# Counting edges of a graph layer with one-hot products: two chunks to a pair, groups of 256 edges, twelve pairs to a batch

## The chip, the core and the metric

The kernel runs on one core of one Trainium2 chip. The metric is the time of one execution on the device in microseconds (us). Before the change three runs gave 567.61, 568.38 and 569.0 us, median 568.38. One more execution was recorded by the hardware profiler; it took 568.89 us, of which 567.1 us are the span that the profile shows.

## The reference

Four residual layers over 1250 nodes with 512 values each: an attention layer over a graph, a gated dense layer, a convolution over the same graph, and a mixture of eight experts. Only the first step matters here. The two graph layers share 40000 edges, whose targets come sorted:

```
dst = minimum(int(1250 * uniform(40000) ** 2.0), 9999);  src = randint(40000, 0, 1250)
order = argsort(dst, stable=True);  src = src[order];  dst = dst[order]
# layer 1: segment softmax over the edges of each target, weighted sum of Wx[src] by target
# layer 3: segment_sum(norm * h[row], col) with the edges and one loop per node
```

The kernel never visits edges again after it has turned them into a matrix C of counts, C[source, target] = how many edges join the two. Both graph layers are then dense products with C.

## The kernel before

Nodes stand in T = 10 tiles of 128 rows (NP = 1280). C has 1280 by 1280 counts in float16, kept in two halves, `C` and `C2`, that take turns and are added at the end of the stage.

**Groups, windows, pairs.** The sorted edges are cut into NG = 105 groups of GE = 384 edges, one group per partition. Targets are cut into NW = 80 windows of WN = 16 targets. As both are sorted, a group meets few windows: there are at most NG + NW - 1 = 184 = NPAIR meetings of a group and a window. Each is a *pair*. A pair has CH = 3 *chunks* of 128 edges. For each chunk VectorE makes a one-hot matrix of the source's low seven bits (128 wide, `L_ring`) and one of source tile and target within the window (RW = 160 wide, `R_ring`). TensorE multiplies them (`count`, line 1445): three products into one PSUM bank. A fourth matmul, the *merge* (line 1452), with the identity as weights, adds what `C` or `C2` holds at that window already. ScalarE writes the sum back (the *write*, line 555). The window's place is a value in a register, different for each pair.

**Order and waits.** Pairs come in batches of LB = 8, 23 batches (NB). The one-hots of a batch (24 chunks) are made in two halves and stand in a ring of two batches. Pair k writes `C` when k is even and `C2` when odd, so merge k waits for the write of pair k-2 (line 1455; `written` counts the writes). `count` of pair k waits, in TensorE's instruction queue, for the write of pair k-3, since three banks take turns (line 1443). In each batch, after the count of pair LB-2, TensorE loads the next batch's windows into registers (line 1520), and ScalarE does so after the write of pair LB-3 (line 606), both in `targets` (line 294).

**What else runs in the stage.** `BEGIN` starts one tile of layer norm in each of batches 1 to 10. Its steps are spread over the next batches: statistics and scale on VectorE (lines 839 to 857), normalization on ScalarE (530, at k = 1), four transposes on TensorE (1356, at k = 2), the copy to float16 on ScalarE (522, at k = 3), the low part on VectorE (862), and then the projection of the attention layer, 12 steps of two matmuls (1402 with 512 columns and 1403 with 16), placed between pairs by `LIN_SLOTS` in batches 3 to 12. VectorE evacuates the result (882, 884). In batches 12 to 15 the weights of the third layer are transposed (1417), copied (628) and split (989). Batch 16 transposes the thresholds of the softmax (1425). Batches 19 and 20 change ScalarE's function tables (lines 542 and 610). In batch 0 small products for the attention scores (1473, 1466) stand between pairs.

**How the pairs are found.** `pair_tables` (VectorE) turns each group's first and last window into selection masks `inside`, `inside_T` and `wneg` over the 184 pairs; `pair_matmuls` (TensorE, lines 1435 to 1439) multiplies the groups' edge values by these masks, so that each partition gets its edge of each pair. ScalarE (line 580) and VectorE (line 930) bring the tables `loT` and `qT` to SBUF. TensorE then transposes weights of layer 1, runs eight matmuls on zeros, and starts to count.

The stage ends when ScalarE has written all pairs and signals `hist_done`; the attention proper starts from that.

Of the kernel before, what the change touches and what calls it, by code (L numbers as in the profile page):

```python
# [22 lines left out]
CH = 3  # L23
GE = CH * P
NG = (EDGES + GE - 1) // GE
GLAST = EDGES - (NG - 1) * GE
# [3 lines left out]
NPAIR = NG + NW - 1  # L30
LB = 8
# [25 lines left out]
LIN_SLOTS = ((0,), (1, 2), (), (3, 4), (5, 6), (7,), (8, 9), (10, 11))  # L57
B_GW = max(BEGIN) + 2
B_CS = B_GW + K
# [6 lines left out]
def gnn_ffn_kernel(nc, x_d, src_d, dst_d, Ws_d, Wb_d, aw_d, ab_d, Wg_d, bg_d, We_d, be_d, gW_d, gb_d,  # L66
                   Wr_d, br_d, W1_d, b1_d, W2_d, b2_d, out_d):
    ctx = ExitStack()
    with ctx:
# [70 lines left out]
        dst_i, o = carve(big, 0, [GE], I32)  # L140
        hi_i, o = carve(big, o, [GE], I32)
# [8 lines left out]
        from_, o = carve(mid, o, [NPAIR])  # L150
        tv, o = carve(mid, o, [NPAIR])
        inside, o = carve(mid, o, [NPAIR], F16)
        inside_T, o = carve(mid, o, [NPAIR], F16)
        wneg, o = carve(mid, o, [NPAIR], F16)
        iota_lo, o = carve(mid, o, [P], F16)
        iota_q, o = carve(mid, o, [RW], F16)
        dst16, o = carve(mid, o, [GE], F16)
        ones16, o = carve(mid, o, [P], F16)
        span_i, o = carve(mid, o, [2], I32)
        num_words = num[:, :, :].rearrange("p h f -> p (h f)")  # L160
        lo16, o = carve(num_words, 0, [GE], F16)
        hi16, o = carve(num_words, o, [GE], F16)
        src_i = be_bc[:, 0:GE].bitcast(I32)
# [59 lines left out]
        ll, at = carve(small, at, [T, H])  # L223
        e1t, at = carve(small, at, [T, H])
# [6 lines left out]
        grp, at = carve(small, at, [8])  # L231
        kt, at = carve(small, at, [MAXPASS])
# [42 lines left out]

        def table_banks(j):

            return (bank[2], bank[3]) if j < 2 else (bank[6], bank[7])
# [42 lines left out]
        def _(sp):  # L321
            sp.wait_ge(sem("pads"), 2)
            full = (NG - 1) * GE
            for i_d, i_sb in ((src_d, src_i), (dst_d, dst_i)):
                sp.dma_start(i_sb[0:NG - 1, :], i_d[0:full].rearrange("(g e) -> g e", e=GE)).then_inc(sem("ld_edges"), 16)
                sp.dma_start(i_sb[NG - 1:NG, 0:GLAST], i_d[full:EDGES].rearrange("(g e) -> g e", g=1)).then_inc(sem("ld_edges"), 16)
# [88 lines left out]
        def _(g):  # L415

            nc.gpsimd.memset(src_i[96:NG, :], 0).then_inc(sem("pads"), 1)
            nc.gpsimd.memset(dst_i[96:NG, :], NP).then_inc(sem("pads"), 1)
# [13 lines left out]
            nc.gpsimd.memset(ones16, 1.0)  # L432
# [79 lines left out]
        def _(a):  # L512
# [63 lines left out]
            def lo_table(p):  # L576

                a.wait_ge(sem("table_psum"), p + 1)
                for n, j in ((2, 0), (1, 2)):
                    ins = act(loT.rearrange("p (k j) c -> p k j c", j=CH)[:, :, j:j + n, :],  # L580
                              bc(table_banks(j)[0][:, 0:NPAIR * n].rearrange("p (j k) -> p k j", j=n), [P, NPAIR, n, 2]), ACT.Copy)
                ins.then_inc(sem("lo_table"), 1)
# [14 lines left out]
            for b in range(NB):  # L597
# [3 lines left out]
                def middle(k):  # L601
# [9 lines left out]
                    if k == 3 and b - 1 in BEGIN:  # L611
# [214 lines left out]
        def _(v):  # L826
# [41 lines left out]
            gp = slice(0, NG)  # L868
            V.tensor_reduce(span_i[gp, 0:1], dst_i[gp, :], AX.X, ALU.min)
            link(V.tensor_reduce(span_i[gp, 1:2], dst_i[gp, :], AX.X, ALU.max))  # L870
            link(V.tensor_scalar(span_i[gp, :], span_i[gp, :], int(math.log2(WN)), None, ALU.logical_shift_right))
            V.tensor_copy(grp[gp, 0:2], span_i[gp, :])
            link(V.tensor_scalar(grp[gp, 2:3], span_i[gp, 1:2], float(NW - 1), 1.0, ALU.min, ALU.add))
            V.tensor_tensor(grp[gp, 2:3], grp[gp, 2:3], grp[gp, 0:1], ALU.subtract).then_inc(sem("n_ready"), 1)
# [476 lines left out]
        def _(pe):  # L1351
# [124 lines left out]
            def between(b, k):  # L1476
# [12 lines left out]
                if k == LB - 2:  # L1489
                    if b - B_GW in range(K):  # L1490
                        second_weights(b - B_GW)
                    if b == B_CS:
                        thresholds()
# [331 lines left out]
```

## Time and profile before

| | |
|---|---|
| median of the runs | 568.38 us (567.61 to 569.0) |
| profiled execution | 568.89 us, its span 567.1 us |
| TensorE matmuls (PE) | 501.0 us busy, 88% |
| VectorE (DVE) | 473.7 us busy, 84% |
| ScalarE (ACT) | 342.2 us busy, 60% |
| one-hots (line 940) | 100 instructions, 92.1 us |
| products (line 1445) | 552 matmuls, 248 ns each |
| merges (line 1452) | shown in one group as 92, 305 ns each; the other 92 stand in a group of their own |

How to read it: busy times are summed over the whole span. A matmul's shown length is its latency; matmuls start sooner than the one before has ended, so a rate is read from the distance of two starts. PEld is the loading of weights. "q" behind an engine's name means its instruction queue. Times of the rows below are us from the start of the span.

### The profile page before, as it was taken

How to read it: one execution, taken by the hardware profiler on the slowest of the kernel's cores; microseconds unless marked ns; L12 is line 12 of the kernel's file. 1: busy time of each engine (PE TensorE's matmuls, PEld its weight loads, DVE VectorE, ACT ScalarE, POOL GpSimd, SP SyncE). 2: the span in 40 equal slices, each digit the busy share in tenths (PEclk: the TensorE clock that was granted, in tenths of full speed). 3: DMA queues.
4: the chain of work that ended last, by engine and by line, in shares of the span. 5: the costliest groups of instructions: out<-in, count | busy, mean ns of one | idle time of the engine just before them, and what ended most of it. 6: DMA issues, size and time to landing. Idle time of an engine off the chain costs nothing.

```text
span 567.1 us, 12112 instructions
## 1 busy us (share of the span) xinstructions
PE 501.0 (88%) x4629; PEld 371.2 (65%) x4630; DVE 473.7 (84%) x933; ACT 342.2 (60%) x662; POOL 72.8 (13%) x83
## 2 busy tenths in 40 slices
PE   1879999887589999999899899989899998899995
PEld 1767777666488888888677544544466696566652
DVE  7999999799899999995898748995877786967681
ACT  5365555567889999994675523344435548756730
POOL 3000000000000000000000020123243410222342
PEclk9989999999899999999999979999999999999999
DMA  7970000002001111100000077000001129675111
GB/s 179 359 273 2 1 2 1 2 10 88 3 39 57 49 49 48 49 3 1 1 1 2 0 253 285 1 1 1 3 21 58 57 65 371 233 248 205 60 52 51
DMA packets 25306, 45.14 MB, mean 80 GB/s; under 512 B 6961, under 2 KB 7205, under 8 KB 25248
## 3 DMA queue, kind: packets, MB, share of 16 engines
q1 hardware_dynamic: 23264, 39.16, 20.2%
q0 software_dynamic: 1952, 5.18, 2.5%
q8 instruction: 39, 0.64, 0.5%
q14 instruction: 19, 0.16, 0.1%
q10 hardware_dynamic: 32, 0.01, 0.0%
HBM read 33.23 MB, written 11.95 MB: 80 GB/s over the span
## 4 chain that ended last, share of the span: by engine, by line
PE 48%; DVE 34%; issue 8%; DMA 4%; ACT 3%; POOL 1%; ACTq 0%; POOLq 0%; DVEq 0%
PE bank L1378 7%; PE bank L1643 5%; PE bank L1767 5%; PE bank L1402 5%; PE bank L1445 4%; DVE work L1072 4%; DVE big L940 4%; PE bank L1452 4%; PE bank L1356 3%; PE bank L1549 3%; PE bank L1562 2%; PE bank L1738 2%; DMA aux<-xperm_scratch 2%; DMA out<-aux 2%; DVE rings L1072 2%
## 5 line engine op out<-in xcount | busy, mean ns | idle before, releaser
L940 DVE TENSOR_TENSOR big<-mid 128x1536 f16<-128x1536 f16 (+1 forms) x100 | 92.1, 980 | 0.4 <-PE bank L1452 0.4
L1445 PE MATMUL bank<-big 128*128 128x160 f16 x552 | 72.1, 248 | 4.4 <-DVE big L940 4.4
L1549 PE MATMUL bank<-big,work 128*128 128x130 f16 x1080 | 67.4, 224 | 8.4 <-DVE work L1072 8.4
L1549 PEld LDWEIGHTS bank<-big,work 128*128 128x128 f16 x1080 | 64.3, 100 | 10.4 <-DVE work L1072 4.9
L1445 PEld LDWEIGHTS bank<-big 128*128 128x128 f16 x552 | 51.7, 111 | 7.0 <-DVE big L940 6.5
L656 ACT ACTIVATE mid<-aux,small 128x1280 f16<-128x1280 f32 x36 | 47.3, 1349 | 0.7 <-DVE work L1072 0.4
L1562 PE MATMUL bank<-big,mid 128*128 128x260 f16 x400 | 47.1, 275 | 0.1
L1643 PE MATMUL bank<-mid 128*128 128x512 f16 x200 | 47.2, 379 | 0.0
L555 ACT ACTIVATE big<-bank 128x160 f32 x92 | 27.9, 303 | 26.7 <-PE bank L1452 25.3
L555 ACT ACTIVATE mid<-bank 128x160 f32 x92 | 27.7, 302 | 25.6 <-PE bank L1452 24.2
L1562 PEld LDWEIGHTS bank<-big,mid 128*128 128x128 f16 x400 | 38.2, 96 | 7.5 <-issue 0.3
L517 ACT ACTIVATE sd<-ve 128x1 f32<-128x1 f32 x40 | 8.0, 200 | 52.8 <-DVE ve L841 52.8
L1402 PE MATMUL bank<-big,rings 128*128 128x512 f16 x120 | 38.6, 378 | 0.0
L472 POOL DMA_INDIRECT out<-aux x16 | 26.3, 1647 | 74.1 <-DVE aux L1294 71.7
L839 DVE BATCH_NORM_STATS2 st<-row 128x6 f32<-128x512 f32 x40 | 27.7, 691 | 8.5 <-POOL row L488 7.8
L1452 PE MATMUL bank<-mid,ident 128*128 x92 | 28.0, 305 | 7.6 <-ACT big L555 4.1
L1549 PE MATMUL bank<-big,rings 128*128 128x130 f16 x520 | 32.0, 220 | 2.5 <-DVE rings L1072 1.6
L530 ACT ACTIVATE rings<-row,nm,rs 128x512 f32<-128x512 f32 x30 | 24.3, 810 | 13.6 <-DVE nm L857 13.6
L1549 PEld LDWEIGHTS bank<-big,rings 128*128 128x128 f16 x520 | 29.9, 98 | 3.6 <-DVE rings L1072 1.9
L456 POOL TENSOR_TENSOR mid<-mid,ident 128x128 f16<-128x128 f16 x10 | 3.9, 424 | 215.9 <-DVE small L1126 215.9
L1643 PEld LDWEIGHTS bank<-mid 128*128 128x128 f16 x200 | 19.7, 104 | 18.1
L1356 PE MATMUL bank<-ident,rings 128*128 128x128 f32 x120 | 19.5, 286 | 12.3 <-ACT rings L530 7.9
(310 smaller groups left out, 1122.1 us busy)
## 6 DMA issues: line engine op xcount, KB each, us to landing
big<-in_L_ffn_W SPq DMA_DIRECT2D x10, 1024.0 KB, 11.0
mid<-in_L_ffn_W SPq DMA_DIRECT2D x6, 1024.0 KB, 13.0
xperm_scratch<-work SPq DMA_DIRECT2D x1, 5753.0 KB, 20.3
aux<-thr_scratch SPq DMA_DIRECT2D x8, 640.0 KB, 3.7
aux<-xperm_scratch SPq DMA_DIRECT2D x8, 523.0 KB, 4.0
row<-in_x SPq DMA_DIRECT2D x1, 2304.0 KB
aux<-in_L_gnn_Ws SPq DMA_DIRECT2D x4, 256.0 KB, 4.5
work<-in_L_gnn_W SPq DMA_DIRECT2D x1, 1024.0 KB, 13.8
```

What stands on the lines that cost most here:

```text
L555: ins = act(counts_at(at[k], k), count_bank(base, k)[:, 0:RW].rearrange("p (d s) -> p s d", s=T), ACT.Copy)
L656: act(zmask[i % NZ], thr_bc[:, h % 2, :], ACT.Sigmoid, bias=steep[:, s, h:h + 1], scale=-STEEP).then_inc(sem("z_made"), 1)
L940: return V.tensor_tensor(out.rearrange("p c (v two) -> p c v two", two=2), values.rearrange("p (v two) -> p v two", two=2).unsqueeze(1).to ...
L1072: V.tensor_tensor(weighted[i % NC], zmask[m % NZ], C[:, s, :], ALU.mult).then_inc(sem("cz_made"), 1)
L1356: ins = nc.tensor.transpose(b[:, k * P:(k + 1) * P], src[:, k * P:(k + 1) * P], ident[:, :])
L1378: ins = mm(out, xt16[:, xp, k, :], w16[:, wp, k, :], start=i == 0 and k == 0, stop=i == 2 and k == K - 1)
L1402: mm(bank[2 + t % 2][:, :], xt, W016[:, wp, k, :], start=j == 0, stop=last)
L1445: mm(count_bank(base, k)[:, 0:RW], L_ring[:, slot, k * CH + j, :], R_ring[:, slot, k * CH + j, :], start=j == 0, stop=False)
L1452: ins = mm(count_bank(base, k)[:, 0:RW].rearrange("p (d s) -> p s d", s=T), ident16[:, :], counts_at(at[k], k), start=False, stop=True)
L1549: ins = mm(acc_region(h, t), weighted[i % NC][:, t * P:(t + 1) * P], VP[:, s, part, h, :, :].rearrange("p b f -> p (b f)"), start=False, s ...
L1562: ins = mm(bank[2 * (t % 2) + g2][:, 0:4 * FE].rearrange("p (h f) -> p h f", f=FE), C[:, s, t * P:(t + 1) * P], VP[:, s, part, 4 * g2:4 * ...
L1643: ins = mm(bank[6 + t % 2][:, :], C[:, s, t * P:(t + 1) * P], hp[:, s, part, :], start=s == 0 and part == 0, stop=s == T - 1 and part == 1)
```

## The change

A group now has 256 edges and two groups stand side by side on one partition (79 partitions, NG = 158). A pair has two chunks. There are 158 + 80 - 1 = 237 pairs, rounded up to 240, in 20 batches of 12. A batch still has 24 chunks, so each instruction that makes one-hots has the shape of before. The masks have a second axis for the two groups of a partition, and each table product is made in two steps, one for each.

```
-CH = 3                                 +CH = 2
 GE = CH * P
-NG = (EDGES + GE - 1) // GE            +ROWE = 2 * GE
                                        +NROW = (EDGES + ROWE - 1) // ROWE
                                        +NG = 2 * NROW
-NPAIR = NG + NW - 1                    +NPAIR = (NG + NW - 1 + LB - 1) // LB * LB
-LB = 8                                 +LB = 12
-LIN_SLOTS = ((0,), (1, 2), (), (3, 4), (5, 6), (7,), (8, 9), (10, 11))
+LIN_SLOTS = ((0,), (1,), (2,), (3,), (), (4,), (5, 6), (7,), (8,), (9,), (10,), (11,))
-B_CS = B_GW + K                        +B_CS = B_GW + K - 1
```

Transposes of a tile move from k = 2 to k = 4, their copy from k = 3 to k = 5, and the thresholds from batch 16, k = 6, to batch 15, k = 4 (they no longer wait for the last split of weights). The loads of windows stay at LB - 3, now k = 9, and bring 12 values. The table code, cut to its core:

```
 def pair_matmuls(p):
     for j in range(CH):
-        mm(lo_ps[:, o], lo16[0:NG, e], inside[0:NG, :], start=True, stop=True)
-        mm(q_ps[:, o], dst16[0:NG, e], inside_T[0:NG, :], start=True, stop=False)
-        mm(q_ps[:, o], hi16[0:NG, e], inside[0:NG, :], start=False, stop=False)
-        mm(q_ps[:, o], ones16[0:NG, :], wneg[0:NG, :], start=False, stop=True)
+        for a in range(2):
+            mm(bank[2][:, o], lo16[gp, e[a]], inside[gp, a, :], start=a == 0, stop=a == 1)
+        for a in range(2):
+            mm(bank[3][:, o], dst16[gp, e[a]], inside_T[gp, a, :], start=a == 0, stop=False)
+            mm(bank[3][:, o], hi16[gp, e[a]], inside[gp, a, :], start=False, stop=False)
+            mm(bank[3][:, o], step16[gp, :], wins[gp, a, :], start=False, stop=a == 1)
 def pair_tables(p):
...
-    V.tensor_scalar(from_[gp, :], iotaK[gp, :], grp[gp, 3:4], None, ALU.is_ge)
+    for a in range(2):
+        V.tensor_scalar(from_[gp, a, :], iotaK[gp, :], first_p[gp, a:a + 1], None, ALU.is_ge)
-    V.scalar_tensor_tensor(inside[gp, :], iotaK[gp, :], grp[gp, 4:5], from_[gp, :], ALU.is_lt, ALU.mult)
+    for a in range(2):
+        V.scalar_tensor_tensor(inside[gp, a, :], iotaK[gp, :], end_p[gp, a:a + 1], from_[gp, a, :], ALU.is_lt, ALU.mult)
...
-    V.tensor_tensor(wneg[gp, :], tv[gp, :], inside[gp, :], ALU.mult)
+    for a in range(2):
+        V.scalar_tensor_tensor(wins[gp, a, :], iotaK[gp, :], off_w[gp, a:a + 1], inside[gp, a, :], ALU.add, ALU.mult)
```

The tables `loT` and `qT` are now brought over by one instruction each instead of two. Ring sizes, the write, the merge and `count` with its waits are as before.

## Rows read from the trace of the kernel before

**Rows 1.** Busy time by stretch: stretch, length, busy PE, PEld, DVE, ACT, POOL (instructions), granted clock, DMA.
```profile
28.50:31.50 3.00, 2.51 (x16) 1.96 (x14) 2.62 (x4) 1.49 (x4) 0.00 (x0) 0.56 1.05 369
41.00:104.40 63.40, 62.39 (x600) 46.45 (x599) 58.92 (x105) 34.96 (x108) 0.00 (x0) 1.00 0.01 2
129.00:147.20 18.20, 13.93 (x144) 11.58 (x144) 17.34 (x22) 13.88 (x44) 0.00 (x0) 1.00 0.12 39
```
**Rows 2.** Chain that ended last, two batches behind the projections: start, length, what.
```profile
115.87 3.87 DVE big L940 x4
...
120.35 3.87 DVE big L940 x4
```
**Rows 3.** Timeline, one batch with a projection, TensorE: start, length, engine, line, operation.
```profile
61.46 0.30 PE L1452 MATMUL bank<-mid,ident 128*128 x1
...
62.07 0.63 PE L1356 MATMUL bank<-ident,rings 128*128 128x128 f32 x4
...
62.53 0.30 PE L1452 MATMUL bank<-big,ident 128*128 x1
...
64.19 0.30 PE L1452 MATMUL bank<-big,ident 128*128 x1
64.28 0.41 PE L1445 MATMUL bank<-big 128*128 128x160 f16 x3
...
64.53 0.38 PE L1402 MATMUL bank<-big,rings 128*128 128x512 f16 x1
...
64.77 0.30 PE L1452 MATMUL bank<-mid,ident 128*128 x1
```
**Rows 4.** Timeline near the stage's end: merges on TensorE and writes on ScalarE.
```profile
142.48 0.30 PE L1452 MATMUL bank<-big,ident 128*128 x1
...
142.81 0.30 ACT L555 ACTIVATE big<-bank 128x160 f32 x1
143.39 0.31 PE L1452 MATMUL bank<-mid,ident 128*128 x1 [0.40 <-ACT big L555]
...
143.73 0.30 ACT L555 ACTIVATE mid<-bank 128x160 f32 x1 [0.61 <-PE bank L1452]
...
144.09 0.31 PE L1452 MATMUL bank<-mid,ident 128*128 x1
```
**Rows 5.** Register loads by line: ns min/median/max, first and last start.
```profile
L294 PEldq TENSOR_LOAD <-mid x23: 587/591/1881, 20.9 to 142.6; - x23
L1522 PEldq TENSOR_LOAD <-small x1: 306/306/306, 146.5 to 146.5; - x1
L294 PEldq TENSOR_LOAD <-mid x1: 592/592/592, 63.3 to 63.3; - x1
```
**Rows 6.** Timeline, making the pair tables: VectorE's first step, first and twelfth table product.
```profile
10.82 0.16 DVE L916 TENSOR_TENSOR small<-small 105x1 f32<-105x1 f32 x1
...
12.85 0.31 PE L1435 MATMUL bank<-mid,num 105*128 105x184 f16 x1 [2.84 <-DVE mid L927]
...
14.49 0.36 PE L1438 MATMUL bank<-mid 105*128 105x184 f16 x1
```
**Rows 7.** Timeline: the merges that begin batches 0, 3 and 13, and the last one.
```profile
22.20 0.30 PE L1452 MATMUL bank<-mid,ident 128*128 x1
...
40.82 0.31 PE L1452 MATMUL bank<-mid,ident 128*128 x1
...
104.40 0.30 PE L1452 MATMUL bank<-mid,ident 128*128 x1
...
146.56 0.30 PE L1452 MATMUL bank<-big,ident 128*128 x1
```
**Rows 8.** Timeline: a weight copy on ScalarE, and the merges around a table change.
```profile
104.11 0.59 ACT L628 ACTIVATE mid<-bank 128x512 f16<-128x512 f32 x1
...
132.01 0.31 PE L1452 MATMUL bank<-mid,ident 128*128 x1
...
133.78 0.31 PE L1452 MATMUL bank<-big,ident 128*128 x1 [1.25 <-ACT big L555]
```

More of the change, by code:

```diff
@@ L22 @@
 EDGES = 40000
-CH = 3
+CH = 2
 GE = CH * P
-NG = (EDGES + GE - 1) // GE
-GLAST = EDGES - (NG - 1) * GE
+ROWE = 2 * GE
+NROW = (EDGES + ROWE - 1) // ROWE
+NG = 2 * NROW
+ELAST = EDGES - (NROW - 1) * ROWE
 WN = 16
@@ L29 @@
 RW = WN * T
-NPAIR = NG + NW - 1
-LB = 8
+LB = 12
+NPAIR = (NG + NW - 1 + LB - 1) // LB * LB
 LC = LB * CH
@@ L223, in gnn_ffn_kernel @@
         ll, at = carve(small, at, [T, H])
+        kt, _ = carve(small, at, [MAXPASS])
         e1t, at = carve(small, at, [T, H])
@@ L230, in gnn_ffn_kernel @@
         steep, at = carve(small, at, [T, H])
-        grp, at = carve(small, at, [8])
-        kt, at = carve(small, at, [MAXPASS])
+        w_lo, at = carve(small, at, [2])
+        w_hi, at = carve(small, at, [2])
+        n_win, at = carve(small, at, [2])
+        first_p, at = carve(small, at, [2])
+        end_p, at = carve(small, at, [2])
+        off_w, at = carve(small, at, [2])
+        n_pass, at = carve(small, at, [1])
         npass, at = carve(small, at, [1], I32)
@@ L578, in lo_table @@
                 a.wait_ge(sem("table_psum"), p + 1)
[L579 to L582, printed above, removed]
+                act(loT.rearrange("p (k j) c -> p k j c", j=CH), bc(bank[2][:, 0:NPAIR * CH].rearrange("p (j k) -> p k j", j=CH),
+                                                                    [P, NPAIR, CH, 2]), ACT.Copy).then_inc(sem("lo_table"), 1)
             for c in range(2):
@@ L610, in middle @@
                         act(sd[0:1, 0:1], zero16[0:1, 0:1], ACT.Sigmoid)
-                    if k == 3 and b - 1 in BEGIN:
+                    if k == 5 and b - 1 in BEGIN:
                         t = BEGIN[b - 1]
@@ L928, in pair_tables @@
+                for a in range(2):
+                    ins = V.scalar_tensor_tensor(wins[gp, a, :], iotaK[gp, :], off_w[gp, a:a + 1], inside[gp, a, :], ALU.add, ALU.mult)
+                ins.then_inc(sem("picks"), 1)
                 v.wait_ge(sem("table_psum"), p + 1)
-                for n, j in ((2, 0), (1, 2)):
-                    V.tensor_scalar(qT.rearrange("p (k j) c -> p k j c", j=CH)[:, :, j:j + n, :],
-                                    bc(table_banks(j)[1][:, 0:NPAIR * n].rearrange("p (j k) -> p k j", j=n), [P, NPAIR, n, 2]),
-                                    0.0, RW + 1.0, ALU.max, ALU.min)
+                V.tensor_scalar(qT.rearrange("p (k j) c -> p k j c", j=CH), bc(bank[3][:, 0:NPAIR * CH].rearrange("p (j k) -> p k j", j=CH),
+                                                                               [P, NPAIR, CH, 2]), 0.0, RW + 1.0, ALU.max, ALU.min)
@@ L1387, in _ @@
             pe.wait_ge(sem("n_ready"), 1)
-            mm(bank[5][0:NG, 0:1], tri[0:NG, 0:NG], grp[0:NG, 2:3], start=True, stop=True)
-            mm(bank[4][0:1, NPAIR:NPAIR + 1], ones[0:NG, 0:1], grp[0:NG, 2:3], start=True, stop=True).then_inc(sem("rb_psum"), 1)
+            gp = slice(0, NROW)
+            for a in range(2):
+                mm(bank[5][gp, 0:1], tri[gp, gp], n_win[gp, a:a + 1], start=a == 0, stop=a == 1)
+            for a in range(2):
+                ins = mm(bank[4][0:1, NPAIR:NPAIR + 1], ones[gp, 0:1], n_win[gp, a:a + 1], start=a == 0, stop=a == 1)
+            ins.then_inc(sem("rb_psum"), 1)
             def lin_a(t, j):
@@ L1479, in between @@
                         lin_a(BEGIN[b - 2], j)
-                if k == 2 and b - 1 in BEGIN:
+                if k == 4 and b - 1 in BEGIN:
                     t = BEGIN[b - 1]
@@ L1488, in between @@
                     score_bias()
[L1489 to L1493, printed above, removed]
+                if k == 4 and b == B_CS:
+                    thresholds()
+                if k == LB - 2 and b - B_GW in range(K):
+                    second_weights(b - B_GW)
             pe.wait_ge(sem("a_spread"), 1)
```

94 lines of the change are left out of this document (47 added, 47 removed).

## The prediction

> **What bounds the kernel now.** I read the page's engine shares first, then the table of busy time by stretch, then the chain that ended last, then the timeline inside single batches. The change touches only the stage that ends at 147 us, so everything behind it counts at nothing: it starts later or earlier by what the stage gives. In the stage two engines are nearly full, which is why the shares alone decide nothing. In the stretch with projections TensorE is busy 62.39 of 63.40 us and VectorE 58.92 [rows 1]; the chain runs through TensorE. Ten batches take 104.40 - 40.82 = 63.58 us [rows 7]. Behind that TensorE's share falls and VectorE is full, 17.34 of 18.20 us [rows 1]; the chain is a row of one-hots, 3.87 us a batch, 4.48 from batch to batch where a weight split stands between [rows 2]. These ten batches take 146.56 - 104.40 = 42.2 us [rows 7].
>
> The reader should see a third limit that no share shows. A merge waits for the write of two pairs before. Merge at 143.39, write at 143.73, end at 144.03, next merge of the same half of C at 144.09 [rows 4]: 0.70 us for two pairs, 0.35 a pair, with no product in that loop. TensorE's own work is nearly as long: merge to first product 0.09, three products 0.25 (0.083 each), so 0.34 [rows 3]. The two limits coincide today. With two products TensorE's own work falls to 0.26, the loop stays at 0.35.
>
> **The change part by part.**
>
> *One-hots.* 23 batches of 3.87 us become 20: VectorE loses 11.6 us of work. That is worth something only where VectorE sets the pace.
>
> *Start.* VectorE turns 512 instead of 384 edges a partition in six instructions. I take 0.1 to 0.16 us each, the growth of 0.35 to 0.56 us instructions by a third, plus one more wait: +0.8. `pair_tables` took from 10.82 to 12.70 (1.9 us) [rows 6]; its instructions over 184 pairs become 240 wide and three of them double: I take +1.3 (bounds 0.9 and 1.9: nothing for width, and all of it doubled). The twelve products start 0.15 us apart, (14.49 - 12.85)/11 [rows 6]: 184 columns at 1.2 GHz. They become 16 of 240 columns, 0.20 each, and the one small product becomes two: 15 x 0.20 + 0.20 against 1.64, +1.6 (bounds 0.4, if the clock were at 2.4 GHz by then, and 1.9). Two evacuations that become one give back some 0.1. All this is a chain, since TensorE's weight transposes, warm-up and first count stand behind the products in its queue. Sum +3.6.
>
> *Batches 0 to 2.* 24 pairs become 36. Twelve more at the loop's 0.35 are 4.2; four pairs beside score products lose 0.08 each, and two later loads grow by 0.16 (next part). Sum +4.1 (bounds 3.1 with the 0.26 of two products, and 6 if the stretch at half clock, 0.56 granted [rows 1], takes in more pairs).
>
> *Ten batches with a projection.* They stay with TensorE. Four more merges at 0.09, as the number of products is the same: +0.37. The transposes now stand at k = 4; at k = 2 they came at 62.07, though merge and products from 61.46 end at 61.80, so they waited 0.27 for ScalarE's normalization [rows 3]. That wait goes: -0.27. The normalization now delays write 2 and by that merge 4: +0.1. Then the register loads. One value took 0.306 us, eight 0.591 [rows 5], so 0.041 a value and twelve 0.75. The load on TensorE can't begin before the wait of the count ahead of it is over: at 63.3 [rows 5], and the matmul behind the load started at 64.53 [rows 3], so there were 1.23 us for 0.59 plus 0.2 until the next matmul (142.6 + 0.59 against 143.39 [rows 4, 5]): 0.43 spare, nothing stalled. After the change two pairs with one projection step each (0.50) stand there instead of two with two (1.66 became 1.0, -0.66), and the load is 0.16 longer: 0.39 short. So +0.4 a batch, between 0 (TensorE's queue covers it) and 0.75. Sum a batch 0.37 - 0.27 + 0.1 + 0.4 = 0.6, ten batches +6.2, bounds 1 and 10.
>
> *The rest.* Seven batches instead of ten. VectorE would need 3.87 to 4.48 each. The loop needs 12 x 0.353, and the load: merge 142.48 to merge 143.39 is 0.91 instead of 0.35, so +0.56 now [rows 4], +0.72 with twelve values. That is 4.96 a batch, more than VectorE's: the loop is late next, not VectorE. Seven are 34.7, less 0.7 for the last, which loads nothing. Work that VectorE's lead hid now shows: the transposes of weights (0.46, as 62.07 to 62.53 [rows 3]) and ScalarE's copies (0.59 [rows 8]) delay the loop by some 0.3 and 0.5 in three batches, 2.7 with the copy at the border; the ten threshold transposes and their copies 1.9; and the two table changes, each 1.77 between merges instead of 0.35 [rows 8], 2.8. Sum 34.0 + 2.7 + 1.9 + 2.8 = 41.4, against 42.2: -0.8 (bounds -11.6, VectorE's three batches, and +3).
>
> The Trainium skill has a rule for the load in "Advanced Engine Details and Errata", section "Sequencer Loop": while the sequencer executes a control instruction, other engine instructions can be read and queued, and its section on queue depths gives TensorE 64 places. By that rule a load would be hidden everywhere. The rows agree where projections fill the queue and disagree behind them, where merges stand 0.91 apart. By the rule alone the sum would be 5 us lower.
>
> *Sum.* 3.6 + 4.1 + 6.2 - 0.8 = +13.1. The profiled execution took 568.89, so 582.0; the median lies 0.5 below it: **581.5 us**.
>
> **The rivals.**
>
> *A. The merge loop and the loads carry the stage, as above:* 581.5, own range 577 to 586. For it: the 0.70 us loop stands in rows without a product in it. Against: it was never longer than TensorE's own work, so it may be a little shorter than it looks.
>
> *B. VectorE goes on setting the pace (the other side).* If the wait of the merge is met early and TensorE runs two products and a merge in 0.26, a late batch needs 12 x 0.26 + 0.72 = 3.84, just under VectorE's 3.87, and the three batches are a full gain of 11.6. Batches 0 to 2 then cost 2.3, those with projections 2 (load hidden), the start 3.6: 568.4 - 3.7 = 564.7. It decides from a pitch under 0.29 us. For it: the two limits coincide, so the rows cannot separate them where nothing stalls. Against: after a stall, merge to write and write to merge are again 0.34 and 0.36 [rows 4].
>
> *C. The loads stay hidden beside projections.* Then these batches cost 0.2 each, and the time is 577.5. For it: today nothing stalls there. Against: the spare 0.43 is used up by the numbers above.
>
> *D. The clock falls.* TensorE idles a quarter of each late pair. Granted clock was 0.56 (the 1.2 GHz level) at 28.5 to 31.5 after a stretch of short products, though TensorE was shown busy [rows 1]. If the 84 late pairs ran at that level, with merges and products twice as long, some 0.13 a pair: +11, 592. For it: the streams get thinner. Against: 1.00 was granted at 129 to 147, with 13.93 of 18.20 us busy [rows 1].
>
> "TensorE: Matmul & The Clock Gate" in the Trainium skill, section "A second HAM failure mode: psum-queue depth-cycling", tells of a kernel whose short idle gaps between groups of matmuls, as it cycled through PSUM banks, made the clock swing between its two levels. Every late pair has such a gap after this change. By that rule D would come; in the trace gaps of 0.4 to 1.2 us between merges left the clock at 1.00.
>
> **How the numbers follow.** A 0.68, C 0.13, D 0.06, B 0.08 (of it 0.05 faster, 0.03 within the bound), and 0.05 for a mix with small loads and less at the start, about 573. Under A, C, D and the mix the time is above 570.1, slower by over 0.3% (1.7 us, about what a measurement of this kernel tells from no change). Slower 0.92, same 0.03, faster 0.05. The range of 8 in 10 takes in A and C and half the mix at the low end, and part of D: 573 to 587.
>
> **What would show it.** Right: one-hots 80 us in total instead of 92.1; merges 0.35 apart behind the projections and ScalarE's writes the releaser of TensorE's idle time; VectorE idle there; first merge at about 25.8, batch 3 at 48.4, batch 13 at 118.5, last merge at 159.5; the load 0.75 us long; late batches 5 us. Wrong: merges 0.26 to 0.29 apart, or VectorE without idle time in the last seven batches (B); batches with projections at 6.6 us and not 7.0 (C); a granted clock under 0.9 behind 118 us (D); a first merge before 24.5.

## The result, and the profile after

The changed kernel takes 588.23 us (median of four runs, 587.49 to 588.63), the one before, timed again beside it, 568.69 (567.61 to 570.79). The ratio on record is 1.0322, 95% interval 1.0289 to 1.0356: slower by 3.2%. (The two medians alone are 3.4% apart.) The forecast was 581.5 with a range of 573 to 587. The direction was right, and 19.5 us came where 13.1 were forecast.

The profiled execution took 588.63 us, its span is 586.9. The merges divide the stage in the same places as [rows 7]. Timeline of the kernel after, the merges that begin batches 0, 1, 3 and 13, and the last one:

```profile
27.68 0.47 PE L1462 MATMUL bank<-mid,ident 128*128 x1
...
42.47 0.42 PE L1462 MATMUL bank<-mid,ident 128*128 x1
...
55.34 0.31 PE L1462 MATMUL bank<-mid,ident 128*128 x1
...
126.31 0.30 PE L1462 MATMUL bank<-mid,ident 128*128 x1
...
166.95 0.30 PE L1462 MATMUL bank<-big,ident 128*128 x1
```

Against [rows 7] this gives a table, in us:

| stretch | before | after | difference | forecast |
|---|---|---|---|---|
| to the first merge | 22.20 | 27.68 | +5.48 | +3.6 |
| batches 0 to 2 | 18.62 | 27.66 | +9.04 | +4.1 |
| ten batches with projections | 63.58 | 70.97 | +7.39 | +6.2 |
| from batch 13 to the last merge | 42.16 | 40.64 | -1.52 | -0.8 |
| from there to the end of the span | 420.54 | 419.95 | -0.59 | 0 |

The forecast missed 6.7 us in sum, and the first two lines alone hold 6.8 of them. What happened there can be read in the timeline of TensorE, kernel after, from the last transposes to the second pair (start, length, line, tiles, count, idle time before and its releaser):

```profile
22.48 1.04 PE L1360 MATMUL bank<-ident,aux 128*128 128x128 f32 x8
27.46 0.43 PE L1455 MATMUL bank<-big 128*128 128x160 f16 x2 [3.95 <-issue]
...
27.87 0.56 PE L1455 MATMUL bank<-big 128*128 128x160 f16 x2
28.22 1.81 PE L1483 MATMUL bank<-aux,work 128*128 128x16 f32 x8
29.86 0.43 PE L1462 MATMUL bank<-big,ident 128*128 x1
```

"issue" means that no semaphore explains the 3.95 us. The register loads do. Those of the whole kernel after (ns min/median/max, first and last start):

```profile
L297 ACTq TENSOR_LOAD <-mid x20: 768/784/2931, 23.6 to 160.4; - x20
L297 PEldq TENSOR_LOAD <-mid x20: 843/852/3032, 24.4 to 160.2; - x20
```

The same view cut to 19 to 30 us leaves TensorE's first one alone:

```profile
L297 PEldq TENSOR_LOAD <-mid x1: 3032/3032/3032, 24.4 to 24.4; - x1
```

The median load answers [rows 5]: 0.852 us for twelve values on TensorE, 0.784 on ScalarE. The first one lasts from 24.4 to 27.4, and the first product starts at 27.46. The clock stands in the busy table of the kernel after (columns as in [rows 1]):

```profile
23.50:27.40 3.90, 0.02 (x1) 0.00 (x0) 3.73 (x11) 0.70 (x2) 0.00 (x0) 0.77 1.06 379
27.50:42.40 14.90, 14.69 (x78) 13.98 (x79) 5.25 (x8) 3.35 (x11) 0.00 (x0) 0.50 0.82 290
43.00:55.30 12.30, 8.71 (x74) 6.09 (x71) 11.37 (x20) 9.12 (x31) 0.00 (x0) 1.00 0.01 2
56.00:126.30 70.30, 67.67 (x637) 51.20 (x634) 57.52 (x100) 44.41 (x144) 0.00 (x0) 1.00 0.01 2
126.30:167.00 40.70, 32.01 (x274) 23.23 (x272) 30.15 (x44) 29.48 (x97) 0.99 (x1) 1.00 0.11 34
```

All of batch 0 runs at a granted clock of 0.50, the 1.2 GHz level. Added up in stretches of 0.25 us, the lower level lasts 17.1 us in this kernel and 3.4 us in the one before, the stretch of [rows 1]. DMA is full (1.06) in the same stretch: the 5.75 MB transfer that zeroes a scratch tensor (from `work` to `xperm_scratch`) begins before the counts and lasted to about 39 us.

In the last line VectorE is busy 30.15 of 40.70 us where it was full before. The chain of waits no longer runs through its one-hots but through TensorE and ScalarE. Timeline of TensorE, kernel after, late in the stage:

```profile
158.93 0.31 PE L1462 MATMUL bank<-mid,ident 128*128 x1
...
159.33 0.31 PE L1462 MATMUL bank<-big,ident 128*128 x1
...
159.63 0.31 PE L1462 MATMUL bank<-mid,ident 128*128 x1
...
160.04 0.31 PE L1462 MATMUL bank<-big,ident 128*128 x1
160.14 0.34 PE L1455 MATMUL bank<-big 128*128 128x160 f16 x2
161.16 0.31 PE L1462 MATMUL bank<-mid,ident 128*128 x1 [0.68 <-ACT big L558]
```

Two pairs take 0.70 us (158.93 to 159.63), 0.35 a pair, as forecast from [rows 4]. (The single distances are uneven, 0.30 and 0.40 here and 0.28 and 0.42 in most late batches, so only the sum of two is to be compared.) Where the load stands, the gap is 1.12 (0.91 in [rows 4]). The one-hots (page of the kernel after) are 80.5 us in 88 instructions, against 92.1, and now wait:

```profile
L944 DVE TENSOR_TENSOR big<-mid 128x1536 f16<-128x1536 f16 (+1 forms) x88 | 80.5, 969 | 11.7 <-PE bank L1462 11.7
```

### The profile page after: what moved, and what is told of

The parts are those of the page before. It is cut to its first block, busy times and chain, and to the rows that moved or that the text cites. A ratio compares the mean times of both kernels' runs of the same rounds, so it can differ in the third digit from the quotient of the medians.

```text
span 586.9 us, 12303 instructions
## 1 busy us (share of the span) xinstructions
PE 515.6 (88%) x4622; PEld 380.1 (65%) x4623; DVE 465.0 (79%) x922; ACT 356.5 (61%) x717; POOL 72.4 (12%) x83
## 3 DMA queue, kind: packets, MB, share of 16 engines
q1 hardware_dynamic: 23212, 39.16, 19.5%
## 4 chain that ended last, share of the span: by engine, by line
PE 56%; DVE 27%; issue 9%; ACT 4%; DMA 2%; POOL 1%; ACTq 0%; POOLq 0%; DVEq 0%
PE bank L1462 7%; PE bank L1382 7%; PE bank L1776 6%; PE bank L1652 5%; PE bank L1455 5%; PE bank L1410 5%; DVE work L1076 4%; PE bank L1747 3%; PE bank L1360 3%; PE bank L1558 3%; PE bank L1571 2%; DVE rings L1076 2%; DVE st L840 1%; DVE work L981 1%; PE bank L1371 1%
## 5 line engine op out<-in xcount | busy, mean ns | idle before, releaser
L944 DVE TENSOR_TENSOR big<-mid 128x1536 f16<-128x1536 f16 (+1 forms) x88 | 80.5, 969 | 11.7 <-PE bank L1462 11.7
L1455 PE MATMUL bank<-big 128*128 128x160 f16 x480 | 81.6, 259 | 3.9 <-issue 3.9
L558 ACT ACTIVATE mid<-bank 128x160 f32 x120 | 36.4, 303 | 32.0 <-PE bank L1462 28.3
L558 ACT ACTIVATE big<-bank 128x160 f32 x120 | 36.5, 304 | 23.2 <-PE bank L1462 22.5
L1462 PE MATMUL bank<-mid,ident 128*128 x120 | 37.4, 311 | 11.2 <-ACT big L558 5.6
L1410 PE MATMUL bank<-big,rings 128*128 128x512 f16 x120 | 44.1, 379 | 2.6 <-issue 2.6
L1462 PE MATMUL bank<-big,ident 128*128 x120 | 36.8, 307 | 1.3 <-ACT big L558 1.3
L533 ACT ACTIVATE rings<-row,nm,rs 128x512 f32<-128x512 f32 x30 | 24.3, 810 | 13.6 <-DVE nm L858 13.6
```

The costliest lines, as they stand in the source:

```text
L558: ins = act(counts_at(at[k], k), count_bank(base, k)[:, 0:RW].rearrange("p (d s) -> p s d", s=T), ACT.Copy)
L944: return V.tensor_tensor(out.rearrange("p c (v two) -> p c v two", two=2), values.rearrange("p (v two) -> p v two", two=2).unsqueeze(1).to ...
L1410: mm(bank[2 + t % 2][:, :], xt, W016[:, wp, k, :], start=j == 0, stop=last)
L1455: mm(count_bank(base, k)[:, 0:RW], L_ring[:, slot, k * CH + j, :], R_ring[:, slot, k * CH + j, :], start=j == 0, stop=False)
L1462: ins = mm(count_bank(base, k)[:, 0:RW].rearrange("p (d s) -> p s d", s=T), ident16[:, :], counts_at(at[k], k), start=False, stop=True)
```

## The experiments

Times of merges below are from the profiled executions, medians and ratios to the kernel before from the timed ones. `a_` stands for a variant of the kernel after, `b_` of the one before. The kernel before was timed again beside each group of variants, there at medians of 570.2 to 570.8 us, so ratios are compared and medians only roughly. A single profiled execution can also lie at the edge of its runs: the one of `a_warm` took 584.25 us where the other three took 586.25 to 587.71, the one of `b_gap` 580.96 where the others took 576.96 to 578.42.

### The late stretch: loop or loads

Four kernels, with part of the work left out. In `a_noloop` and `b_noloop` merges add zeros instead of C and wait for no write, so TensorE needs no register; ScalarE's write waits for the one two back. In `a_noload` the merge reads C at one fixed place, so TensorE loads nothing but waits as before. In `a_loadonly` only the first and last merge of a batch are real, so the loads stay and the loop goes.

```
 a_noloop, b_noloop:
-  ins = mm(count_bank(base, k)..., ident16[:, :], counts_at(at[k], k), ...)
+  ins = mm(count_bank(base, k)..., ident16[:, :], zero16[:, 0:RW]..., ...)
-  if isinstance(base, int) and base + k > 1:
-      ins.wait_op(sem("written"), base + k - 1, "sem-ge")
 and in the write, on ScalarE:
+  elif base + k >= 2:  a.wait_ge(sem("written"), base + k - 1)
 a_noload:
-  ... ident16[:, :], counts_at(at[k], k), ...
+  ... ident16[:, :], (C, C2)[k % 2][:, :, 0:WN], ...
 a_loadonly: as a_noloop, but only for 0 < k < LB - 1
```

> The changed kernel with the merge reading zeros instead of C and not waiting for the write of two pairs before (the sums over pairs of one window are left out; every matmul and write stays). Theory 1, the loop of merge and write carries the late stretch: merges fall from 0.353 to 0.29-0.31 apart (the three PSUM banks bind next), the late batches from 5.1 to some 4.3 us, time 579 to 583. Theory 2, TensorE's rate or the register loads carry it: merges stay 0.35 apart, 587 to 589.

> The same edit in the kernel of before, with its three products to a pair. Theory 1: the loop does not bind there, VectorE and TensorE do: 567 to 569, no change of note. Theory 2, the loop costs something with three products as well: 563 to 566.

> The changed kernel with every merge reading window 0 of its half of C, its wait kept, so that TensorE loads no registers (which windows are summed is left out; ScalarE still loads its own and writes as before). The run without loop and loads took 574.1, 14.1 less than the changed kernel. Theory 1, the loop is the larger part in the late stretch: late stretch 38 to 39 us (40.6 in the changed kernel, 35.3 without both), merges 0.35 apart; the first merge comes at 24.6 as there, since the 3 us load goes; projections 68 to 69 us for 71.0; 576 to 580. Theory 2, the loads were nearly all of it: late stretch 36 us, 574 to 575.

> The changed kernel with ten of twelve merges reading zeros without a wait (sums over pairs of a window are left out for these), the first and last of a batch reading C as before, so that TensorE keeps its register loads. Theory 1: first merge at 27.7 and batch 0 at the low clock as in the changed kernel; late stretch 37 to 39 us, projections 70 to 71; 582 to 586. Theory 2, loads alone: as the changed kernel, 587 to 589.

| kernel | median us | ratio (interval) | first merge | batch 3 | batch 13 | last | projections | late |
|---|---|---|---|---|---|---|---|---|
| after | 588.23 | 1.032 (1.029 to 1.036) | 27.68 | 55.34 | 126.31 | 166.95 | 70.97 | 40.64 |
| `a_noload` | 578.38 | 1.015 (1.010 to 1.019) | 24.45 | 50.60 | 118.15 | 156.02 | 67.55 | 37.87 |
| `a_loadonly` | 586.02 | 1.027 (1.022 to 1.031) | 28.02 | 55.04 | 125.64 | 163.67 | 70.60 | 38.03 |
| `a_noloop` | 574.08 | 1.008 (1.005 to 1.011) | 24.59 | 48.71 | 116.14 | 151.39 | 67.43 | 35.25 |
| `b_noloop` | 568.02 | 0.996 (0.993 to 0.999) | 20.36 | 40.11 | 103.63 | 144.77 | 63.52 | 41.14 |

The table is a square of two causes. In the late stretch the loop costs 2.6 us (40.64 - 38.03; 37.87 - 35.25) and TensorE's loads cost 2.8 (40.64 - 37.87; 38.03 - 35.25); both are real and they add up. Neither edit takes its cause out whole: `a_loadonly` keeps the wait in two merges of twelve, and `a_noload` keeps ScalarE's load, so that at the end of each of its batches 16 to 18 a distance of 0.90 us between merges is left where the kernel after has 1.12. Beside projections the loads cost 3.2 to 3.4 (70.60 - 67.43; 70.97 - 67.55) and the loop 0.1 to 0.4. To the first merge the loads cost 3.2 (27.68 - 24.45), and 1.5 in batches 0 to 2. In the kernel before, loop and TensorE's loads together are worth 1.0 us in the late stretch (42.16 - 41.14): VectorE is last there, as busy there as ever. Busy table, `b_noloop`, the stretch from batch 13 on:

```profile
103.60:144.80 41.20, 32.22 (x341) 26.56 (x339) 40.70 (x56) 28.12 (x93) 0.98 (x1) 1.00 0.09 35
```

So the mechanism of rival B is real only without loop and loads: then the late stretch is 35.25 us, 6.9 shorter than before. Against what was expected: `a_noload` (37.87 and 67.55), `a_loadonly` (38.03 and 70.60) and `b_noloop` came out by their first theories, the stretches to within 0.5 us. `a_noloop` came out 5 us under its range of 579 to 583, since its edit took TensorE's loads away as well, which its expectation had not reckoned with.

### The wait in front of the load

`a_waitop` moves the wait of the count from TensorE's queue onto its first product, so that a load behind it needn't stand behind a wait.

```
-  at_least(pe, "written", base + (k - 2) ...)
+  if j == 0 and isinstance(base, int) and base + (k - 2) > 0:
+      ins.wait_op(sem("written"), base + (k - 2), "sem-ge")
```

> The changed kernel with the count's wait for the write of three pairs before attached to its first matmul instead of standing in TensorE's queue, so that the queue can run ahead and read the register load early. Theory 1, the load is late because it stands behind that wait: the 0.25 us of idle time in each batch with a projection goes (2.5 us in ten batches) and the gap of 1.1 us between the merges around a load in the late batches shrinks to the 0.42 of its neighbours (6 x 0.7 = 4 us): 581 to 584. Theory 2, the load itself blocks TensorE wherever it stands, or ScalarE's own load ends last: 587 to 589.

Nothing moved: 588.04 us, ratio 1.032 (1.025 to 1.039), last merge at 167.12, the distance around a late load 1.12 as before. The place of this wait was not the cause. The merge ahead of the count waits for the same write; that it holds the load back just as well is my reading, and no run tries it.

### The start: the gap and the clock

`a_warm` puts 22 matmuls on zeros behind the last transposes, where TensorE stood idle. `b_gap` gives the kernel before such a gap (a wait for the one-hots of half of batch 1), and `b_gap_warm` the gap with 28 matmuls in it. `a_noscore` leaves the weights' products for the attention scores out of the kernel after.

```
 a_warm, b_gap_warm, behind w0_T(3):
+  for _ in range(22):      (28 in b_gap_warm)
+      mm(bank[5][:, 0:400], zero16[:, 0:P], zero16[:, 0:400], start=True, stop=True)
 b_gap, b_gap_warm, ahead of at = targets(mybir.EngineType.PE, 0):
+  pe.wait_ge(sem("onehots"), LB + LB // 2)
 a_noscore, in the pair loop:
-  if b == 0 and k < K:
-      weights_of(k)
```

> The changed kernel with 22 matmuls on zeros (400 columns each) queued behind the last weight transpose, so that TensorE runs while the first register load (3.0 us) goes on. Theory 1, the clock fell in the 3.95 us gap before the first count and stayed at the 1.2 GHz level for batch 0: granted clock 1.00 from 23.5 to 42 us, score products 0.84 us a group instead of 1.60, last merge 5 to 6 us earlier than 166.95, time 582 to 583. Theory 2, batch 0 is slow for another reason (DMA traffic, the products themselves) and the gap only happens to be there: clock 0.5 in batch 0 as before, time 588 to 589.

> The kernel of before, where TensorE waits ahead of the first register load until VectorE has made the first half of batch 1 as well: first merge at 24.8 to 25.5 instead of 22.2, an idle gap of some 4.5 us as the changed kernel has. Theory 1, such a gap drops the clock and the small products that follow keep it down: score groups 1.6 us instead of 0.84, batch 1 at 36 to 38 (30.67 before), last merge 4 to 7 us later than 146.56, 572 to 576. Theory 2, the gap costs only its length and VectorE's lead takes that up: batch 1 at 33.5, 568 to 571.

> The same wait with 28 matmuls on zeros queued ahead of it, so that TensorE runs through the gap. Theory 1: the clock stays at 1.00 through the score products, batch 1 at 33 to 35, 569 to 572, at least 2 us less than without them. Theory 2: equal to the kernel with the bare wait.

> The kernel after with the weights' products (score products, the weights' transposition and what reads them in batch 0) left out. Theory 1 (the small 16-column products keep the granted clock at the lower level): the clock is back at 1.00 within batch 0, the counts of batch 0 go at 0.28 to 0.35 us a pair, and batch 1's merge comes 5 to 7 us after the first one, near 33 to 35 us. Theory 2 (the idle time before batch 0 alone puts the clock down and counts at the lower clock don't bring it back): the clock stays near 0.50 to about 40 us, pairs go 0.5 us apart, and batch 1 comes near 35 to 37 us, batch 3 near 50.

| kernel | median us | ratio (interval) | first merge | batch 1 | batch 3 | last |
|---|---|---|---|---|---|---|
| `a_warm` | 586.57 | 1.029 (1.022 to 1.037) | 27.61 | 38.38 | 51.36 | 163.16 |
| `a_noscore` | 584.71 | 1.024 (1.020 to 1.029) | 27.64 | 38.06 | 52.27 | 164.0 |
| `b_gap` | 577.98 | 1.011 (1.008 to 1.013) | 27.35 | 40.68 | 51.88 | 157.43 |
| `b_gap_warm` | 577.75 | 1.010 (1.006 to 1.013) | 27.14 | 39.13 | 50.14 | 155.67 |

Busy tables, `a_warm` first:

```profile
24.00:28.00 4.00, 3.80 (x27) 2.20 (x24) 3.83 (x11) 0.29 (x2) 0.00 (x0) 1.00 1.05 379
28.00:32.50 4.50, 4.50 (x47) 4.50 (x46) 2.71 (x5) 1.22 (x5) 0.00 (x0) 1.00 1.07 376
32.70:40.00 7.30, 6.22 (x34) 5.38 (x33) 3.67 (x4) 3.50 (x9) 0.00 (x0) 0.54 0.89 318
```

and `a_noscore`:

```profile
23.50:27.40 3.90, 0.08 (x1) 0.01 (x1) 3.73 (x11) 0.77 (x2) 0.00 (x0) 0.79 1.07 376
27.50:45.90 18.40, 14.82 (x81) 13.13 (x81) 12.66 (x18) 8.64 (x25) 0.00 (x0) 0.50 0.68 243
```

Idle time without any score product goes ahead of a fall: in `a_noscore` the clock is at 0.50 right behind a gap of 3.84 us, and at the lower level for 20.5 us in all, to 46.3. So does a run of score products without idle time: in `a_warm` the clock is 1.00 through them and 0.54 behind them, and the lower level lasts 6.8 us. That the products themselves bring it down is not shown, since no run leaves out both them and the gap. Theory 1 for `a_noscore`, that the clock would come back within batch 0, is wrong; theory 2 has the clock right and the times too early (batch 1 at 38.06, batch 3 at 52.27), since the low clock lasted longer than it assumed. For `a_warm` theory 1 holds in part: score groups at 0.85 us, but a clock of 1.00 only up to 32.5 us and not 42, and 3.8 us instead of 5 to 6 at the last merge. The filling is worth 4.1 us at batch 1 and 4.0 at batch 3 in the profile, but 1.7 us in the medians, inside its interval.

`b_gap` has the clock and the slow score groups of its theory 1, and more time than that allowed (batch 1 at 40.68, 577.98 us). `b_gap_warm` did not keep the clock up, as its busy table shows:

```profile
24.00:28.50 4.50, 2.25 (x22) 1.79 (x20) 3.57 (x6) 0.30 (x1) 0.00 (x0) 1.00 1.05 377
28.50:45.50 17.00, 16.26 (x93) 15.49 (x92) 8.34 (x12) 6.18 (x18) 0.00 (x0) 0.50 0.64 229
```

The matmuls on zeros took off only the first part of the low stretch, 17.1 us of it instead of 23.9, so the 0.2 us between the two medians are not the price of a clock that stays up. Theory 2 of `b_gap_warm`, equal to the bare wait, has the time.

### The start: the transfer and the score products

Two edits, alone and together, on both kernels. `_score` makes the score products ahead of batch 0, where TensorE stood idle, rather than between its pairs. `_defer` lets the zeroing transfer wait until 36 pairs (24 in the kernel before) are counted; `b_score_late` waits for 104.

```
 _score:
-  if b == 0 and k < K:  weights_of(k)
-  if b == 0 and k == K:  score_bias()
 and ahead of batch 0:
+  for k in range(K):
+      weights_of(k)
+  score_bias()
 _defer, on SyncE ahead of the transfer to xp_d:
+  sp.wait_ge(sem("counted"), 36)
```

> The changed kernel with the five groups of small score products (16 columns) moved from between the pairs of batch 0 to behind the last weight transpose, into the time of the first register load. Theory 1, the gap and these products drop the clock, and the 3 us load can cover them: batch 1 begins at 33 to 36 instead of 42.5, 579 to 583. Theory 2, DMA traffic or VectorE holds batch 0 back: batch 1 after 40, 586 to 588.

> The changed kernel with the transfer that zeroes the scratch tensor (5.75 MB) held back until 36 pairs are counted. Theory 1, the first register load takes 3.0 us because of DMA traffic: it takes 0.85 to 1.5 us, first merge at 25.5 to 26.2, the gap is 2 us and the clock holds for the score products, 580 to 584. Theory 2, it is slow because it is the first of its kind (code or addresses not at hand): 3.0 us as before, 588.

> The kernel after with the score products ahead of batch 0 and the zeroing transfer held back past batch 3. Theory (the start's excess over my forecast is the slow first register load plus the score products at the lower clock): batch 1 comes near 33 us, batch 3 near 46 to 47 against 55.3 of the kernel after; the projection stretch then takes about 74.5 us (the transfer lies there), the late one 40.6, and the median is 583 to 586. Rival: the gap before batch 0 alone sets the clock and the start: batch 3 near 50 and the median 587 to 588.

> The same move in the kernel of before. Theory 1: its first load took 1.0 us, so the products delay the first merge to 24.5 and free batch 0: batch 1 at 29 to 30.7, batch 3 within 1 us of 40.8, and the late stretch is VectorE's: 567 to 569. Theory 2: the clock no longer falls, 564 to 566.

> The kernel of before with the score products moved ahead of the first count and the zeroing transfer held back until 24 pairs are counted. If DMA traffic slows the loads of batches 1 and 2 (1.9 and 1.3 us for 0.59), batch 3 comes 1 to 2 us earlier than in the kernel with the move alone (40.43): 565 to 567.5, faster than before. If not: as that kernel, 567 to 569.

> The kernel before with the score products of the weights ahead of batch 0 and the zeroing transfer held until the stretch in which VectorE sets the pace (104 pairs counted). Theory: the transfer costs time only by making the register loads slow where TensorE waits for them; in the late stretch VectorE's one-hots are last, so slow loads are hidden there. Then batch 3 starts merging near 37.8 us, batch 13 near 101 (projection batches at 6.36 us), the last merge near 143.5, and the median is 564.5 to 567. Rival: the transfer costs its 3.3 us wherever it lies, because the loads also hold late batches: batch 13 near 101 but the last merge near 146.5 and the median 568 to 570.

| kernel | median us | ratio (interval) | first merge | batch 1 | batch 3 | batch 13 | last |
|---|---|---|---|---|---|---|---|
| after | 588.23 | 1.032 (1.029 to 1.036) | 27.68 | 42.47 | 55.34 | 126.31 | 166.95 |
| `a_score` | 585.13 | 1.025 (1.022 to 1.029) | 28.87 | 36.13 | 50.13 | 121.06 | 161.92 |
| `a_defer` | 588.09 | 1.029 (1.026 to 1.033) | 25.32 | 37.27 | 50.32 | 124.91 | 165.74 |
| `a_score_defer` | 584.27 | 1.025 (1.020 to 1.030) | 27.53 | 33.48 | 46.28 | 120.36 | 161.11 |
| `b_score` | 568.42 | 0.997 (0.994 to 0.999) | 23.89 | 29.72 | 40.43 | 103.97 | 145.99 |
| `b_score_defer` | 568.77 | 0.996 (0.993 to 0.998) | 23.67 | 28.43 | 37.83 | 104.69 | 146.69 |
| `b_score_late` | 569.16 | 0.998 (0.996 to 1.001) | 24.3 | 28.71 | 38.33 | 103.2 | 146.55 |

TensorE's first register load in `a_defer`:

```profile
L297 PEldq TENSOR_LOAD <-mid x1: 1038/1038/1038, 24.1 to 24.1; - x1
```

Its timeline right behind that load:

```profile
25.18 0.30 PE L1456 MATMUL bank<-big 128*128 128x160 f16 x2 [1.92 <-issue]
25.32 0.30 PE L1463 MATMUL bank<-mid,ident 128*128 x1
```

Same instruction, same twelve values, same place: 3.03 us beside the transfer, 1.04 without it. The first merge comes at 25.32 instead of 27.68. Hence 2.0 of the 5.5 us at the start are the transfer's effect on one load.

Full DMA alone does not do this. In the kernel before the first load took 1.04 us while DMA was as busy; its load, and its busy table:

```profile
L294 PEldq TENSOR_LOAD <-mid x1: 1043/1043/1043, 20.9 to 20.9; - x1
20.00:22.00 2.00, 0.07 (x1) 0.03 (x1) 1.90 (x7) 0.76 (x2) 0.00 (x0) 1.00 1.05 385
```

That was other traffic: in `b_score_late`, where the transfer waits, the DMA share falls from 1.23 at 22.0 to 22.5 us to 0.31 at 23.0 to 23.5. So what the change did is move the load from 20.9 to 24.4, from ahead of the transfer into it.

The load came out by theory 1 of `a_defer`, the time by theory 2: 588.09 us, nothing gained. Batch 3 comes 5.0 us earlier, batch 13 only 1.4. Two things stood against a gain. Busy table of `a_defer`, the start and then behind the transfer's new place:

```profile
25.00:28.50 3.50, 3.32 (x34) 3.33 (x34) 3.43 (x6) 0.91 (x3) 0.00 (x0) 1.00 0.01 3
28.50:39.00 10.50, 9.74 (x53) 8.76 (x52) 6.00 (x9) 4.19 (x10) 0.00 (x0) 0.51 0.01 2
60.00:62.00 2.00, 2.00 (x11) 1.35 (x10) 2.00 (x5) 1.29 (x3) 0.00 (x0) 0.50 1.06 378
```

The gap ahead of the first count is 1.92 us, as long as in the kernel before (1.93), and yet the lower level lasts 10.2 us against 3.4. And batches 3 and 4, beside the transfer now, take 8.87 and 8.92 us instead of 7.1: one load takes 2.63 us, and behind it the clock is at the lower level once more. `a_score` came near its theory 1 at batch 1 (36.13 for 33 to 36) and missed its time (585.13 for 579 to 583): the clock fell twice, for 3.4 us at 28.5 and for 6.8 at 35.5.

Busy table of `a_score_defer`:

```profile
23.50:28.00 4.50, 4.50 (x44) 4.50 (x44) 4.33 (x12) 0.49 (x2) 0.00 (x0) 1.00 0.05 8
28.00:32.00 4.00, 4.00 (x26) 3.61 (x25) 3.93 (x7) 2.45 (x9) 0.00 (x0) 0.57 0.02 4
32.00:46.00 14.00, 9.84 (x84) 6.99 (x83) 12.40 (x21) 10.12 (x34) 0.00 (x0) 1.00 0.01 2
```

With both edits the lower clock lasts 3.4 us, as in the kernel before, and batch 3 comes at 46.28, 9.1 us earlier than in the kernel after and 2 earlier than my forecast. Each edit alone gives 5 of them. All that its theory named came out: batch 1 at 33.48, projections 74.08, the late stretch 40.75, 584.27 us.

The time improves by less, 4.0 us in the medians and 4.6 in the spans (586.9 to 582.3), and the profile says where most of the rest went: the transfer now lies beside projections, and its price comes back through the loads. The projections' group on TensorE (columns: busy us, mean ns, idle time before and its releaser) between batches 3 and 13, kernel after:

```profile
L1410 PE MATMUL bank<-big,rings 128*128 128x512 f16 x119 | 43.7, 379 | 2.6 <-issue 2.6
```

The same group in `a_score_defer`:

```profile
L1411 PE MATMUL bank<-big,rings 128*128 128x512 f16 x119 | 43.7, 379 | 5.7 <-issue 5.7
```

The matmul behind a load idles 5.7 us instead of 2.6, and the stretch grows by the same 3.1 (74.08 against 70.97). Two loads there took 2.67 and 2.12 us. Another 1.2 us went behind the stage (421.2 us from the last merge to the end, 419.95 in the kernel after), which nothing here explains.

`b_score` came out by its theory 1 (568.42 us); its clock fell all the same, at 24 us, behind the score products. `b_score_defer` came out by its mechanism and not by its time: batch 3 at 37.83, 2.6 us earlier than in `b_score`, but 568.77 us, since batches 3 and 4 take 8.91 and 7.21 us instead of 6.4, with loads of 1.77 and 1.88.

`b_score_late` was to put the transfer where VectorE's lead hides slow loads. It did not pay: 569.16 us, the rival's number. Three TensorE loads took 1.77 to 1.94 us, and the distances between merges around them are 2.03, 2.13 and 2.21 where `b_score` has 0.7 to 0.9, some 4 us in sum. The late stretch grew by 1.3 only (43.35 us against 42.02 in `b_score`), so VectorE's lead did hide most of it. And the 2.1 us that this kernel led `b_score` by at batch 3 had shrunk to 0.8 at batch 13, with no transfer near. There TensorE waited for VectorE, as its groups in `b_score_late` from 38 to 104 us show:

```profile
L1403 PE MATMUL bank<-big,rings 128*128 128x512 f16 x120 | 38.6, 378 | 1.2 <-DVE rings L863 1.2
```

The line answers to one with no idle time in the kernel before. The wait is a single one, in the first pair of batch 3: 1.93 us from merge to merge where `b_score` takes 0.59, for the low part that VectorE makes (line 863). TensorE was early there and VectorE was not. `b_score` and `b_score_defer` are the complete kernels that come out ahead of the one before, by 0.3 to 0.4%, with intervals that exclude no change; against its three first runs (568.38) the same medians show nothing.

## Why the prediction was right in direction and short in size

**Start (forecast +3.6, measured +5.48).** The part that I had worked out holds: TensorE's first register load began at 24.4 against 20.9 [rows 5], +3.5, and the table products start 0.20 apart. What failed is that the first load itself had no term. I priced loads at 0.75 from the medians (they measured 0.85, since twelve values cost more than a straight line through one and eight says) and had the maximum of 1.88 in the same row [rows 5] without asking when it came. It comes at 26.8 us, beside the transfer. The first load took 3.03 us where the first one before took 1.04: +2.0, shown by `a_defer` and from the other side by `a_noload`. The +3.5 that I had forecast are what pushed it there. The reading "184 columns at 1.2 GHz" has no row for it: the granted clock was 1.00 from 12.8 to 14.9 us. The distance grew with the columns, 0.15 to 0.20, and that alone carried the sum.

**Batches 0 to 2 (forecast +4.1, measured +9.04).** This is the step that failed most. I took twelve pairs at 0.35 and the clock as it was. Batches 1 and 2 did that: 12.87 against 10.15, +2.7, for eight pairs. Batch 0 took 14.79 against 8.47, +6.3. Its five pairs with score products took 10.72 us against 5.97, since at the 1.2 GHz level eight such products need 1.6 us instead of 0.84, and its other seven pairs took 4.07, mostly 0.53 apart. My bound of 6, for the case that the stretch at half clock takes in more pairs, was the right mechanism, but it reckoned with counts at half clock and not with the score products. In the trace this is a chain: slow load, 3.95 us without a matmul, clock at 0.50 for the whole batch. `a_defer` and `a_score`, which shorten or fill the gap, each take 5 us off batch 3, both together 9.1. But the load and the gap are not all of the low clock: with neither of them long (`a_defer`) it still lasted 10.2 us, three times as long as before the change. The step that failed is the clock taken as it was; what sets the length of the low stretch stays open.

**Ten batches with a projection (forecast +6.2, measured +7.39).** Right in kind and in its terms: 7.1 us a batch where 7.0 was forecast. The distance between merges around the load is 0.93 where its neighbours have 0.52, so the load costs 0.4 in a batch, as I took it; 0.25 of it shows as idle time of TensorE (2.6 in ten, with "issue"). By the rule of the Trainium skill ("Advanced Engine Details and Errata", "Sequencer Loop"), as I read it, the load would be hidden behind queued matmuls; it is not, as the 0.25 us of idle time in each batch show, and rival C is out: `a_noload` puts the loads' price in this stretch at 3.4 us.

**The rest (forecast -0.8, measured -1.52).** Right: 0.35 a pair, VectorE with idle time, 4.93 us in batch 17, which has nothing else in it, where 4.96 was forecast. The load adds 1.12 - 0.35 = 0.77 where I took 0.72; of that the square above gives 0.46 (2.8 us over six batches) to TensorE's own load, with ScalarE's left in place. Of the 0.7 us that the stretch came out better by, 0.35 is a slip of mine: from the first merge of batch 13 to the last of all there are 83 distances, and I counted 84. B is out. Its mechanism needs both loop and loads gone.

**Rival D.** Wrong where I put it: the granted clock was 1.00 over 126 to 167 us, with TensorE busy 32.01 of 40.70. The Trainium skill's account of idle gaps between groups of matmuls ("TensorE: Matmul & The Clock Gate", "A second HAM failure mode: psum-queue depth-cycling") would have had it swing there, and this trace doesn't show it. But a fall of the clock did cost about 5 us (10.72 - 5.97 in five pairs), at the start, where I had reckoned with the 3 us at the lower level that [rows 1] shows.

**What stays open.** Why the clock comes back after 3.4 us in the kernel before and in `a_score_defer`, after 6.8 in `a_warm` and 10.2 in `a_defer`, and only after 17 to 24 us in the kernel after, `b_gap_warm`, `a_noscore` and `b_gap`. It fell behind idle time and behind score products, but no run here separates what takes it down or keeps it down. Idle time does not always do it: TensorE stood still beside slow loads in `a_defer` and in `a_score_defer` alike (0.08 of 2 us busy at 56, 0.07 at 52), and the clock fell behind the one and not behind the other. That this transfer slows register loads was seen wherever the two met; by what path was not tried.

## What to carry to other kernels

Read the maximum of a register load beside its median, and ask what traffic lies there: a load that stands alone ahead of a phase is a term of its own, and a change that delays it can move it into a transfer that it used to miss. Price a delay at the start of a phase with the clock that follows from it, and with every matmul of the first batch at that clock, not only those that the change adds. When a transfer is moved out of the way, look for what waits on a register where it lands.

## What the runs showed that I had not expected

- A load of twelve values from SBUF into TensorE's registers takes 0.85 us with DMA quiet, 1.04 at the start with the transfer held back, and 3.03 beside it; eight values 0.59 and up to 2.10 (`b_gap`). Other traffic that filled the DMA queues just as well left the first load of the kernel before at 1.04.
- TensorE's clock fell to the 1.2 GHz level behind runs of 16-column float32 matmuls at which TensorE was shown busy throughout (4.50 of 4.50 us in `a_warm`).
- A gap of 7.66 us instead of 1.93 on TensorE ahead of the first count (`b_gap`) put batch 3 11.1 us later (51.88 against 40.82), about twice what the gap had grown by: the clock stayed at 0.50 from 24 to 47.8 us. That is the profiled execution, the slowest of its four; the ratio of the runs (1.011) puts the price at some 6 us of the whole time.
